# Moving three links of a chain between TensorE, ACT and VectorE to earlier places in a hand-written order

## What is computed

```python
q = _rope(proj(Wq, bq), e)
k = _rope(proj(Wk, bk), e)
v = proj(Wv, bv)
scale = jnp.sqrt(jnp.asarray(dh, x.dtype))
att = jnp.einsum('bhqd,bhkd->bhqk', q, k) / scale
causal = jnp.tril(jnp.ones((t, t), dtype=bool))
att = jnp.where(causal[None, None], att, -jnp.inf)
att = jax.nn.softmax(att, axis=-1)
y = jnp.einsum('bhqk,bhkd->bhqd', att, v)
y = y.transpose(0, 2, 1, 3).reshape(b, t, e)
return jnp.einsum('bte,fe->btf', y, Wo) + bo
```

## Time and profile before

| what | value |
|---|---|
| time, median of 3 runs | 6254.84 us (6247.21 to 6261.84) |
| profiled execution: its own time | 6254.84 us |
| profiled execution: span from first to last instruction | 6253.2 us |
| mean granted TensorE clock | 0.809 of full speed |
| TensorE busy, span's share | 4620.3 us, 74% |
| VectorE busy | 3743.1 us, 60% |
| ScalarE busy | 1854.3 us, 30% |
| GpSimd busy | 2168.6 us, 35% |

### The profile page before, as it was taken

How to read it: one execution, slowest core, us unless ns; L and a number is a source line. 1 busy time by engine, 2 the same in 40 slices (tenths; PEclk the granted TensorE clock), 3 DMA queues, 4 the chain that set the end, 5 groups by cost and what they waited for, 6 DMA issues and landing times. The chain is left out here.

```text
span 6253.2 us, 94417 instructions
## 1 busy us (share of the span) xinstructions
PE 4620.3 (74%) x35752; PEld 2773.9 (44%) x35752; DVE 3743.1 (60%) x11081; ACT 1854.3 (30%) x2829; POOL 2168.6 (35%) x2704
## 2 busy tenths in 40 slices
PE   5979797979697877767768667587676775876763
PEld 3444545454445453443534535335344354353442
DVE  3555555555555555448567676576676755866764
ACT  2424242424243333333123232231232322312320
POOL 1323131313131313556135253261352522613425
PEclk9989898989898988887768778687687677876876
DMA  4000000000000000650000000000000000000000
GB/s 141 7 17 7 16 8 15 10 13 11 12 11 12 12 12 30 205 166 8 9 19 2 15 13 6 16 8 10 19 3 15 11 6 17 6 12 17 3 15 4
DMA packets 141904, 146.45 MB, mean 23 GB/s; under 512 B 31262, under 2 KB 126048, under 8 KB 141048
## 3 DMA queue, kind: packets, MB, share of 16 engines
q1 hardware_dynamic: 114280, 93.48, 5.1%
q0 software_dynamic: 18432, 37.79, 1.9%
q10 hardware_dynamic: 8736, 8.91, 0.4%
HBM read 69.64 MB, written 62.59 MB: 21 GB/s over the span
## 5 line engine op out<-in xcount | busy, mean ns | idle before, releaser
L792 DVE CUSTOM_DVE_ANT_0 twin<-twin,w_mask_row 128x512 f32<-128x512 f32 (+3 forms) x2048 | 952.0, 522 | 339.4 <-PE twin L1752 337.6
L1752 PE MATMUL twin<-arena 32*128 32x128 f32 (+3 forms) x4096 | 824.9, 528 | 51.6 <-DVE arena L792 27.4
L1770 PE MATMUL twin<-arena 32*128 32x128 f32 (+3 forms) x4096 | 787.3, 499 | 53.7 <-DVE arena L792 51.1
L1435 ACT ACTIVATE arena<-twin 128x768 f32<-128x768 f32 (+1 forms) x544 | 478.3, 880 | 711.5 <-PE twin L1781 387.9
L1770 PEld LDWEIGHTS twin<-arena 32*128 32x128 f32 x4096 | 346.8, 196 | 485.8 <-issue 266.4
L695 POOL TENSOR_SCALAR ve<-mv 128x4 f32<-128x4 f32 x128 | 27.5, 215 | 1513.6 <-DVE mv L752 1513.0
L1752 PEld LDWEIGHTS twin<-arena 32*128 32x128 f32 x4096 | 361.0, 207 | 234.6 <-issue 109.1
L321 POOL DMA_INDIRECT got<-sorted_y,back x288 | 280.6, 974 | 531.7 <-ACT ring L1641 262.7
L313 POOL DMA_INDIRECT sorted_x<-got,w_mo_first_slots x288 | 281.6, 978 | 470.2 <-DVE ring L866 300.7
L1705 PE MATMUL twin<-w_ident,b 128*128 128x128 f32 x328 | 88.8, 431 | 342.0 <-DVE b L773 336.4
L1793 PE MATMUL twin<-arena 128*32 128x128 f32 (+3 forms) x2944 | 304.4, 457 | 23.7 <-POOL arena L597 23.7
(11 more groups left out here) (440 smaller groups left out, 10460.0 us busy)
## 6 DMA issues: line engine op xcount, KB each, us to landing
sorted_y<-arena SPq DMA_DIRECT2D x96, 256.0 KB, 2.8
sorted_x<-zeros ACTq DMA_DIRECT2D x2, 4096.0 KB, 20.0
a<-sorted_x SPq DMA_DIRECT2D x64, 128.0 KB
b<-sorted_x SPq DMA_DIRECT2D x64, 128.0 KB, 2.6
hres<-sorted_x SPq DMA_DIRECT2D x64, 128.0 KB
sorted_x<-got,w_mo_first_slots POOLq DMA_INDIRECT x288
got<-sorted_y,back POOLq DMA_INDIRECT x288, 2.5
x_out<-w_l_w SPq DMA_DIRECT2D x18, 256.0 KB, 2.3
```

Of the source, the lines that this page charges most:

```text
L792: last = dve.tensor_tensor_reduce(s[:, e, at:at + w], s[:, e, at:at + w], W["mask_row"][:, T - w:T], -1.0, 3e38, ALU.add, ALU.min, into)
L1435: act.activation(at_pt[tag][n % len(at_pt[tag])][:, :, 0:w], twin[SLOT["scores_t", c, u] % 3][:, :, 0:w], ACT.Exp, scale=1.0 if tag == "l1 ...
L1752: last = pe.matmul(s[:, e, at:at + w], queries[r, P * i:P * (i + 1)], keys[r, 0:w], start=(at == 0), stop=True, skip_group_check=True)
L1770: last = pe.matmul(s[:, e, at:at + w], keys[r, P * m:P * (m + 1)], queries[r, P * m:T], start=(at == 0), stop=(tag == "l2"), skip_group_ch ...
```

## The change

Three conditions in the hand-written order of the twin attention, all of them for the tag "l2" alone. `divide(c - 1)` on DVE goes from u = 5 to u = 3 of step c, `invert(c - 1)` on ACT from u = 3 to u = 2, and `spread_sums(c - 1)` on PE from u = 3 to u = 2. Each of these calls still stands behind the maxima, the exponent or the scores of its u. The waits within the functions stay as they are.

```diff
--- before.py
+++ after.py
@@ -822,7 +822,7 @@
                                     beside(c, u)
                                     if tag == "l2" and u == 1:
                                         shift(c + 1)
-                                    if u == (2 if tag == "l1" else 5):
+                                    if u == (2 if tag == "l1" else 3):
                                         divide(c - 1)
 
                         def l0_attention():
@@ -1473,7 +1473,7 @@
                                         take_max_rows(c + 1)
                                     if tag == "l2" and u == 1:
                                         take_values(c - 1)
-                                    if tag == "l2" and u == 3:
+                                    if tag == "l2" and u == 2:
                                         invert(c - 1)
 
                         def top2_exp(q, ex, w):
@@ -1876,7 +1876,7 @@
                                     elif u == 1:
                                         turn_max(c + 1)
                                         values(c - 1, 2)
-                                    elif u == 3:
+                                    elif u == 2:
                                         spread_sums(c - 1)
                                     elif u == 4:
                                         values(c, 0)
```

## The result

The changed kernel takes 6303.44 us in the median of 6 runs (6293.46 to 6327.52), the kernel before 6247.98 us in 6 runs beside them (6232.44 to 6261.84). The ratio of the two is 1.0103, with a 95% interval of 1.0079 to 1.0128: 1.03% slower (the quotient of the two medians is 1.0089), where 0.34% was forecast, and above the range. The profiled execution took 6302.32 us, with a span of 6300.7 us and a granted clock of 0.804.

A forecast was written before the change was run, and what follows sets the result against it. Steps 1 to 5 were taken as bound by VectorE's queue plus waits TensorE causes, the tail by its dependency chain; 14.4 + 18.0 - 11.3 = +21.1 us on 6254.84 gave 6276 us, 0.34% slower, range 6243 to 6300.

The forecast's parts named there:

- The division: VectorE's division in steps 1 to 5 finds its inverse ready; moving it frees and costs nothing, 0 us.
- The queue order: Scores and exponent of u=3 queue behind sums and inverse; VectorE loses 0.45 us in each of four steps, +14.4 us.
- The waits that go: Shorter TensorE gap before values(c, 1) removes VectorE waits of steps 1 to 5; at most 12.9 us, credited 11.3.
- have the same look: VectorE's other waits between shift(2) and divide(4), 12.9 us in all, come from 1.2 GHz behind the gap before values(c, 1).
- The gap that grows: Longer TensorE idling before the sums lowers the clock in steps 1 and 3; 8 x (0.6 + 0.9) x 1.5 = +18.0 us.
- The fifth step "covered": Step 5's loss hides in VectorE's existing wait of 1.2 to 3.5 us at shift(7), so costs nothing.
- the tail 0: Step 7 and the last step: scores only pair otherwise, 1 us over all pairs at most, counted 0.
- 0.1 us later at most: Step 7: scores of u=2 go alone, 3 and 4 pair; 0.1 us later at most, 1 us over all pairs.
- Rival 1: Clock holds through the longer gaps in front of the sums; only +1.5 us left, 6256 us; chance 0.25.
- Rival 2: Step 5's pushed-back work fills the gap before values(5, 1), tail regains full clock; -12.5 us, 6242 us; chance 0.13.
- Rival 3: Clock falls last two or three stretches, 3.5 us each, 8 x 1.5 falls; +45 us, 6300 us; chance 0.20.

The follow-up runs named there:

- experiment 2: Against the kernel before, only the division moved, to u=3; ratio 1.0002.
- experiment 3: The whole change plus 2, 3, 2 and 3 extra unread products before the wait for the shift in steps 1, 3, 4, 5; ratio to before 1.0011.
- experiment 1: Against the kernel before, only TensorE's sum product moved, to u=2; inverse and division stay; ratio 1.0105.
- experiment 9: Against the kernel before, all three moves made in step 6 alone; ratio 1.0012.
- experiment 10: Against the kernel before, all three moves made in steps 7 and 8 alone; ratio 0.9998.
- experiment 12: Against before: the change, head work at u=2, step 6's inverse and sums at u=3, two extra products before sums of steps 2 and 5; 0.9973, 6252.82 us.

## Why the prediction was wrong

The sign, the mechanism and most of the place were right; the sizes of two terms were not.

- **The division, 0.** Right (experiment 2).
- **The queue order, +14.4 us (0.45 in each of four steps).** Right. Step 2 takes 12.7 us in the five pairs of before that have full clock in it, and 13.2 in seven pairs of after: 0.5 us. With the gap filled (experiment 3), VectorE waits 0.34 us at the maxima of u = 4 wherever the clock is full, and for nothing at u = 3 (0.1 was forecast). The stage is 3.7 us longer there, where 14.4 - 12.9 = 1.5 was the sum for full clock; the scatter doesn't tell the two apart.
- **The waits that go, -11.3 us.** Right in kind: VectorE waits 6.3 us in nine waits at the maxima of u = 1 of steps 3 and 4 in before, and 0.7 us in one in after. But not all of the 12.9 us "have the same look": 2.9 of them are waits at u = 2 and 4 of step 2, in three pairs, in a 1.2 GHz stretch that reaches over from step 1. They go as well, so that step 2 is only 0.8 us longer over eight pairs (105.7 to 106.5).
- **"The gap that grows", +18.0 us: the step that failed.** The clock's part is what after has over experiment 3: 16.5 us in step 1, 14.8 in step 3 and 12.1 in step 4, together 43.4. The prediction had 0.6 x 8 falls in step 1, 0.9 x 8 in step 3 and none in step 4, at 1.5 us each: 7.2, 10.8 and 0. The trace has 8, 8 and 7 falls, and 23 falls of 1.5 us would have been 34.5, so the count carried most of the error.

  The largest part, 12.1 of the 25.4 us that were missing, is step 4, whose gap was taken as 1.5 us and left out. It is 2.5 to 3.0 us in seven pairs. Two terms that aren't independent meet there. In the first pair of before the scores of u = 1 in step 4 run at 1.2 GHz (1.23 us where they take 0.70 in after), and VectorE waits 1.05 us for them. With that gone ("the waits that go") TensorE is early, and idles for longer in front of the sums. This is read from the rows of one pair; no run tests it.

  In step 1 the gap was sized rightly (2.3 forecast, 2.27 in the row), with a chance of 6 in 10 to lower the clock; experiment 1, where the same gap lowered it in two pairs of seven, shows that such a gap can go either way, so that eight falls out of eight may be in part chance. The price per fall was 43.4 / 23 = 1.9 us; most low stretches of step 1 last 6.8 us and catch three waits of VectorE, not two.
- **The fifth step "covered", and the tail 0: wrong together by 9.7 us** (329.8 to 339.5). Two things that the profile shows. First, the cover: the prediction argued from the GpSimd product that starts in step 5 before the loss, and left out the second one of that step, which waits for a `take` behind the delayed maxima. GpSimd in the first pair of after; in before this product followed its mask without a wait:

```profile
2957.97 5.47 POOL L651 TENSOR_TENSOR w_mo_wgu<-w_mo_wgu 128x2048 f32<-128x2048 f32 x1 [1.10 <-DVE absorbed_q L1367]
```

  The masks of the last steps follow it, so `values(6, 0)` waits for longer, and the clock falls there too. TensorE and the granted clock of after, beside the earlier trace rows:

```profile
2964.22 0.62 PE L1793 MATMUL twin<-ring,arena 128*32 128x512 f32 x2 [2.07 <-POOL ring L597]
...
2965.23 2.10 PE L1770 MATMUL twin<-arena 32*128 32x256 f32 x12
```

```profile
2965.20:2968.50 3.30, 3.30 (x24) 1.41 (x20) 1.31 (x2) 1.57 (x2) 0.93 (x2) 0.50 0.02 5
```

  Seven of the eight pairs have the product's wait of 1.1 us, and in five of them `values(6, 0)` waits 2.07 to 2.09 us; in before one pair waited there, 1.28 us. Second, "0.1 us later at most" holds where the clock is full in step 6, and not where a 1.2 GHz stretch reaches into it (experiment 9). It was said of step 7, where it is right (experiment 10); step 6, where the clock is low in the earlier trace rows, was not looked at.

  Of the pairs of after, five are of the first kind (22.6 us each from `shift(7)` on) and three of the second (22.0, 22.0 and 22.3), where the mean of before is 20.7; from the start of step 5 to `shift(7)` it is 4 us less than in before, over eight pairs. Both belong to the gaps. In experiment 3, with all three moves in place and the gaps filled, the stretch from step 5 to `divide(7)` is 328.1 us, 1.7 less than before, and the second product of step 5 waits in no pair. The nearest of these gaps is the one in front of the sums of step 5, which the prediction called covered. Experiment 3 fills those of steps 1, 3 and 4 as well, so that it is this one alone isn't shown for this kernel.
- **Rival 1, the clock holds**, gave 6256 us. It is refuted by the granted clock of every first step of after, and experiment 3 is what it would have looked like. Single gaps of 2.27 us can leave the clock full (experiment 1), but not the gaps of 4.2 us and more in step 3.
- **Rival 2, the tail gets its clock back**, was wrong, though `shift(7)` now waits 7.9 us in three pairs where it waited 24.5 in eight, and for the reason it named: the gap in front of the sums of step 5 leaves the clock low (0.50 from 2948.1 to 2954.9).
- **Rival 3, the falls last longer (6300 us)**, is the nearest to the result, at 3 us. But it is not how the time came about: it had 12 falls of 3.5 us, the trace has 23 of 1.9 and 10 us of tail.

## What to carry to other kernels

Before an instruction is moved ahead of others in a queue, work out what the engine has left to do while that instruction waits; here the scores of u = 3 were the cover of the wait for the shift, and taking them away cost more in granted clock than in waiting. Then go through the terms once more as if the others had already come true: the low clock that went away in one place was what had kept the gap of step 4 short. When the wait can't be shortened, put work whose result nobody needs into it (1.0103 to 1.0011), or better, move what delays the awaited instruction: with the head work behind the shift the same change cost nothing (0.9973 in one kernel, 0.9992 in a close variant of it). And where a loss is called covered, check every transfer or product of that stretch, not the one that comes first.

## What was not expected of the hardware

- Extra matmuls made the kernel faster with no other edit in the stage: in experiment 12, 6252.82 us against 6266.75 without them (ratios to before of 0.9973 and 0.9992, whose intervals overlap a little); in experiment 3 against the change, 1.0011 and 1.0103.
- Of the 24 gaps ahead of the sums in steps 1, 3 and 4 of after, the 23 of 2.27 us and more were followed by 1.2 GHz, always with products right before and right behind. Experiment 1 has gaps of 2.27 us that were not, five of seven in step 1. So the same gap can go either way.
- The length of the gap doesn't give the length of the low stretch either. In after a gap of 2.27 us (step 1) left 6.8 us in seven pairs of eight, one of 4.2 us (step 3) 3.4 us in five pairs of six, and the two of 4.9 us 10.2 us each.
- Being busy didn't bring the clock back at once: in the fifth pair of experiment 9 TensorE was busy for 6.50 of 6.50 us at 0.50.
